# Attention output stored by accumulating DMAs onto the tokens in memory, so that the second scoring pass and the second feed-forward read one tensor

## The chip, the cores and the metric

The kernel runs on one core of one Trainium2 chip. The metric is the time of one execution on the device in microseconds. The time before is the median of three runs, 4940.31 us (4940.25 to 4942.61).

## The reference, cut to what matters

```python
def reference(x, ...):                       # x: 8 x 2048 x 256, float32
    x = x + 0.5 * ffn(layernorm(x), ...)     # first half block
    x = x + attention(layernorm(x), ...)     # 8 heads of 32 channels
    x = x + 0.5 * ffn(layernorm(x), ...)     # second half block, same weights

def ffn(x, w_router, W_qkv, W_out, g1, g2, W1, W2, W3):
    scores = x @ w_router                    # one number per token
    idx = top_k(scores, 128)                 # 128 of 2048 tokens per batch row
    x_sel = x[idx]                           # only these go through
    ...                                      # causal attention and gated FFN on 128 tokens
    return x with the rows idx replaced      # all other rows pass unchanged
```

The attention block's residual sum `x + attention(...)` is the one that the change moves. Each half block is also a pass over all 16384 tokens, since y = x + 0.5 * layernorm(x) for the tokens that are not picked.

## The kernel before, in words

Eight stages follow each other, each closed by a barrier of all engines (`cleared_semaphores`): `score_pass` s1, `pick_tokens` t1, `routed_ffn` f1, `project` pr, `attend` at, `score_pass` s2, `pick_tokens` t2, `routed_ffn` f2. The names of tiles begin with the stage (the profile drops the digit, so `s_x` is the tile x of s1 and s2).

**score_pass** (line 65) goes over 16 groups of 1024 tokens, four buffers deep. SP loads a group (1 MB, line 129), VectorE takes statistics and the router's product of each of its 8 tiles (lines 174 and 178) and then works out scale and bias in some 17 small dependent steps on 128x8 numbers (lines 184 to 205), ScalarE writes y (line 220) and issues its store (line 224). With `add` given, SP also loads the same group of a second tensor (line 132) and GpSimd adds it to the first in two halves (line 156); VectorE waits for each half. s1 is called without `add`; s2 adds `attention` to `after_ffn`.

**routed_ffn** (line 390) gathers the picked rows, 128 per batch row, with GpSimd's indirect DMAs (line 548), and with `add` a second gather and a GpSimd sum for each (lines 551 and 556). VectorE waits for the weights, which SP loads, and then for the rows (line 604). f1 is called without `add`, f2 with `attention`.

**attend** (line 1218) works in 64 units, 8 batch rows times 2 groups of four heads times 4 blocks of 512 queries. A unit has 16 cycles on TensorE (line 1676), one for each chunk c of 128 keys. A cycle computes the four heads' scores (line 1658), which ScalarE exponentiates into `probs` (line 1561, a ring of 8 chunks of 1 MB each), multiplies the chunk before with v (`pv`, line 1622) and computes one scores tile for the next units' row maxima (line 1589, reduced by VectorE in line 1462).

The sum of the exponentials over keys is shared. Chunks 13 and 15 are summed on TensorE. Ten others are added in pairs by accumulating DMAs from SBUF to SBUF, issued from GpSimd's queue (`start_pair`, line 1419): pairs (3,4), (5,6), (7,8), (9,10), (11,12). Pair d waits for TensorE to have passed chunk c of the pair (`pv_done`, line 1417). GpSimd adds what is left in eight adds of 128x2048 (line 1442), n = 0 to 7. The adds n = 2 to 6 take the results of pairs 0 to 4 and wait for their landing (`dma_added`, line 1430). GpSimd's order in a unit is written out: add 0, add 1, pairs 0 and 1, add 2, pair 2, add 3, pair 3, add 4, pair 4, adds 5, 6 and 7.

In cycle 3 of the next unit TensorE waits for the eighth add and closes the sum (`close_z`, line 1638). Turned and inverted, it scales the output in cycle 6 (`normalize`, line 1490), which fills `o`, of which there are two buffers, and raises `o_done`. SP waits for that and stores `o` into the tensor `attention` (`store`, line 1351): 256 KB in 512 rows of 128 channels, that is 512 B each, four to a partition. Between the stores SP issues the loads of queries, keys and values and the row maxima.

Of the kernel before, what the change touches and what calls it, by code (L numbers as in the profile page):

```python
# [15 lines left out]
P = 128  # L16
F32 = mybir.dt.float32
# [3 lines left out]
ALU = mybir.AluOpType  # L21
# [3 lines left out]
B, S, D = 8, 2048, 256  # L25
# [1183 lines left out]
RAW_CHUNKS = (13, 15)  # L1209
DMA_PAIRS = ((3, 4), (5, 6), (7, 8), (9, 10), (11, 12))  # L1210
DMA_BEFORE_ADD = (2, 2, 3, 4, 5)
CLOSE_Z_IN = 3
TURN_Z_IN = 4
TURN_O_IN = 6
# [3 lines left out]
def attend(nc, tag, qk, v_dram, out):  # L1218

    UQ = 512  # L1220
    NU = S // UQ
# [26 lines left out]
    with ExitStack() as ctx:  # L1248
# [63 lines left out]
        def _(sp):  # L1312
# [30 lines left out]
                                 .rearrange("a h (t q) -> a (h t) q", q=P),  # L1343
                                 max_row[first * QT:end * QT].bitcast(F32)).then_inc(max_in, 16)

            def store(unit, b, un):

                g, u = un // NU, un % NU
                sp.wait_ge(o_done, unit + 1)
                sp.sem_inc(load_turn, 1)  # L1350
                sp.dma_start(out[bass.ds(b * S + u * UQ, UQ), g * P:(g + 1) * P].rearrange("(t p) c -> p t c", p=P),
                             o[:, un % 2].rearrange("p t h d -> p t (h d)")).then_inc(o_out[un % 2], 16)

            load_q(0, 0)
            load_kv(0, 0)
            load_q(0, 1)
# [4 lines left out]
            def batch(b, first_batch=False, last=False):  # L1361

                for un in range(BU):
                    unit = b * BU + un
                    if un + 3 < BU or not last:

                        sp.wait_ge(scores, unit * TILES)
                        sp.sem_inc(load_turn, 1)
                        load_q(b + (un + 3) // BU, (un + 3) % BU)
                    if un == 0 and not first_batch:  # L1370

                        sp.wait_ge(pv_done, unit * NC)
                        sp.sem_inc(load_turn, 1)
                        load_kv(b, 1)
                    if un == NU and not last:

                        sp.wait_ge(pv_done, unit * NC)
                        sp.sem_inc(load_turn, 1)
                        load_kv(b + 1, 0)
                    if un > 0:  # L1380
                        store(unit - 1, b, un - 1)
                    elif not first_batch:
                        store(unit - 1, b - 1, BU - 1)
                    if un + 1 < BU or not last:
                        row_of_max(unit + 1, un + 1)
                if last:
                    store(b * BU + BU - 1, b, BU - 1)

            batch(0, first_batch=True)
            with sp.Fori(1, B - 1) as b:  # L1390
                batch(b)
            batch(B - 1, last=True)
            for k in range(2):
                sp.wait_ge(o_out[k], B * BU // 2 * 16)


        @block.gpsimd
        def _(pool):
# [7 lines left out]
            for first, end in ((0, HG - 1), (HG - 1, HG)):  # L1406
                to = SHIFT_AT[first]
                nc.gpsimd.memset(ks[to:to + 1, :, first:end].bitcast(F32), 1.0).then_inc(ones_row, 1)

            def batch(b, first_batch=False):  # L1410
                for un in range(BU):
                    unit = b * BU + un
# [7 lines left out]
                                            ).then_inc(dma_added[(un * ND + d) % 2], 16)  # L1420

                    for n in range(ADDS):
                        for d in range(ND):
                            if DMA_BEFORE_ADD[d] == n:
                                start_pair(d)
                        c = pool_chunks[n + 1]
                        paired = [d for d in range(ND) if DMA_PAIRS[d][1] == c]
                        if paired:
                            k = un * ND + paired[0]
                            pool.wait_ge(dma_added[k % 2], (b * (BU * ND // 2) + k // 2 + 1) * 16)  # L1430
                        else:
                            pool.wait_ge(exp_done, unit * TILES + c * HG + HG)
                        if n == 0:
                            if un > 1 or not first_batch:

                                pool.wait_ge(z_done, unit - 1)
                            a = probs[:, pool_chunks[0] % RING]
                        else:

                            pool.wait_ge(pool_added, unit * ADDS + n)  # L1440
                            a = acc
                        nc.gpsimd.tensor_tensor(acc, a, probs[:, c % RING], ALU.add).then_inc(pool_added, 1)  # L1442

            batch(0, first_batch=True)
            with pool.Fori(1, B) as b:
                batch(b)


        @block.vector
# [273 lines left out]
def macaron_block(nc, x, qU, qVt, qb, kU, kVt, kb, vU, vVt, vb, w_router, w_qkvT, w_outT, g1, g2, w1T, w2T, w3T,  # L1723
                  out):
    after_ffn = nc.dram_tensor("after_ffn", [B * S, D], F32).ap()
    attention = nc.dram_tensor("attention", [B * S, D], F32).ap()
    scores = nc.dram_tensor("router_scores", [P, P], F32).ap()
    qk = nc.dram_tensor("qk_parts", [B, 2, 2 * NG, P, S], F32).ap()
    v_dram = nc.dram_tensor("v_tokens", [B * S, D], F32).ap()
# [1 line left out]
    with nc.sbuf_tensor("picked", [P, B], U32) as picked:  # L1731
        score_pass(nc, "s1", x, None, w_router, after_ffn, scores)
        pick_tokens(nc, "t1", scores, picked[:])
        routed_ffn(nc, "f1", x, None, picked[:], *ffn_weights, after_ffn)
        project(nc, "pr", after_ffn, [(qU, qVt), (kU, kVt), (vU, vVt)], [qb, kb], vb, qk, v_dram)
        attend(nc, "at", qk, v_dram, attention)
        score_pass(nc, "s2", after_ffn, attention, w_router, out, scores)
        pick_tokens(nc, "t2", scores, picked[:])
        routed_ffn(nc, "f2", after_ffn, attention, picked[:], *ffn_weights, out)


# [32 lines left out]
```

## Time and profile before

| what | value |
|---|---|
| median of 3 runs | 4940.31 us |
| time of the profiled execution | 4941.97 us |
| its span, first to last instruction | 4940.2 us |
| mean granted TensorE clock | 0.933 |
| PE busy | 3962.8 us (80%) |
| DVE busy | 3256.7 us (66%) |
| ACT busy | 2839.3 us (57%) |
| POOL busy | 2797.0 us (57%) |
| DMA moved | 676.10 MB, mean 137 GB/s |

PE is TensorE, DVE VectorE, ACT ScalarE, POOL GpSimd, and SP the engine that issues most loads. The shares are means over the eight stages, of which attend takes some 3440 us, from 935 us to 4378 us of the span; the other stages have other limits. A wait is put down to the semaphore that came last. q0 is the DMA queue of the transfers that GpSimd issues, q1 that of SP, q10 that of ScalarE. All of them use the same 16 DMA engines.

### The profile page before, as it was taken

The numbers are of one execution on the slowest core, as the hardware profiler recorded it, in microseconds if no ns is written. First come the engines' busy times: TensorE is split into PE (matmuls) and PEld (weight loads), VectorE is DVE, ScalarE is ACT, GpSimd is POOL, SyncE is SP. The second block draws the span as 40 slices with busy tenths as digits, with TensorE's granted clock in tenths as the row PEclk, the third lists the DMA queues.
The fourth block names the chain that finished last, engine by engine and source line by source line (L and its number), as shares of the span: only waits on it lengthen the run. The fifth ranks groups of instructions, "written<-read, shape, count | busy, mean of one in ns | idle before, by whom it ended". The sixth has DMA issues, their size and how long they took to land. (4 is left out here: it accounts for less than half of the span.)

```text
span 4940.2 us, 69035 instructions
## 1 busy us (share of the span) xinstructions
PE 3962.8 (80%) x21362; PEld 1555.6 (31%) x21362; DVE 3256.7 (66%) x3736; ACT 2839.3 (57%) x5625; POOL 2797.0 (57%) x966
## 2 busy tenths in 40 slices
PE   0156476499999999999999999999999999930166
PEld 0134354133333333333333333333333333310144
DVE  8744365577767767776776776677677777549644
ACT  4143355266666666666666666666666666634043
POOL 0011000277777777777777777777777777753111
PEclk9999788699999999999999999999999999965599
DMA  6200499556676675766667575676657666467200
GB/s 222 76 29 5 149 353 328 113 124 139 131 157 134 136 154 110 158 127 144 146 132 151 108 163 122 138 157 128 144 119 162 129 138 129 92 192 246 78 5 5
DMA packets 316558, 676.10 MB, mean 137 GB/s; under 512 B 24780, under 2 KB 208608, under 8 KB 268832
## 3 DMA queue, kind: packets, MB, share of 16 engines
q0 software_dynamic: 48000, 340.81, 34.0%
q1 hardware_dynamic: 234624, 297.04, 20.9%
q10 hardware_dynamic: 33568, 33.69, 2.0%
q8 instruction: 191, 3.13, 0.3%
q14 instruction: 175, 1.43, 0.1%
HBM read 198.90 MB, written 136.48 MB: 68 GB/s over the span
## 5 line engine op out<-in xcount | busy, mean ns | idle before, releaser
L1462 DVE TENSOR_REDUCE at_part_max<-at_ps_max 128x4 f32<-128x2048 f32 x1024 | 2347.7, 2293 | 1022.6 <-PE at_ps_max L1589 1021.6
L1561 ACT ACTIVATE at_probs<-at_ps_s 128x512 f32<-128x512 f32 x4096 | 2233.4, 596 | 1045.3 <-PE at_ps_s L1658 989.8
L1442 POOL TENSOR_TENSOR at_pool_sum<-at_pool_sum,at_probs 128x2048 f32<-128x2048 f32 x448 | 2055.7, 4589 | 289.9 <-DMA at_probs<-at_probs 277.3
L1658 PE MATMUL at_ps_s<-at_qs,at_ks 97*128 97x512 f32 (+1 forms) x4096 | 1715.8, 472 | 72.0 <-ACT at_probs L1561 36.3
L1658 PEld LDWEIGHTS at_ps_s<-at_qs,at_ks 97*128 97x128 f32 (+1 forms) x4096 | 683.0, 188 | 1496.9 <-ACT at_probs L1561 1208.1
L1622 PE MATMUL at_ps_acc<-at_probs,at_v 128*32 128x512 f32 x8192 | 1098.0, 608 | 0.9 <-ACT at_probs L1561 0.9
L1589 PE MATMUL at_ps_max<-at_ks,at_qs 32*128 32x512 f32 x4096 | 525.2, 501 | 89.8 <-DVE at_part_max L1462 43.3
L1419 POOL DMA_DIRECT2D at_probs<-at_probs x320 | 282.0, 881 | 494.8 <-PE at_ps_acc L1622 465.9
L1442 POOL TENSOR_TENSOR at_pool_sum<-at_probs 128x2048 f32<-128x2048 f32 x64 | 292.2, 4566 | 98.7 <-ACT at_probs L1561 98.7
L1589 PEld LDWEIGHTS at_ps_max<-at_ks,at_qs 32*128 32x128 f32 x4096 | 198.1, 183 | 444.0 <-DVE at_part_max L1462 296.6
L238 PE MATMUL s_pt<-s_ident,s_sall 128*128 128x128 f32 x2 | 0.9, 447 | 359.5 <-DVE s_sall L205 359.5
L1622 PEld LDWEIGHTS at_ps_acc<-at_probs,at_v 128*32 128x32 f32 x8192 | 161.5, 108 | 257.3 <-issue 248.3
L1399 POOL MEMSET at_ones<- 128x128 f32 x1 | 0.2, 204 | 337.3 <-POOLq L62 337.3
L220 ACT ACTIVATE s_y<-s_x,s_small 128x256 f32<-128x256 f32 x256 | 129.2, 587 | 59.1 <-DVE s_small L201 59.1
L1187 PE MATMUL pr_pqk<-pr_xT,pr_w 128*128 128x512 f32 x256 | 132.3, 665 | 37.1 <-DVE pr_lo L1090 34.0
L565 POOL TENSOR_TENSOR f_att<-f_att,f_rowsum 128x1280 f32<-128x1280 f32 x16 | 49.5, 3096 | 172.3 <-DVE f_rowsum L650 172.3
L1630 PE MATMUL at_ps_misc<-at_probs,at_ones 128*32 128x512 f32 x1024 | 137.0, 607 | 0.0
L156 POOL TENSOR_TENSOR s_x<-s_x,s_add 128x1024 f32<-128x1024 f32 x32 | 74.3, 2342 | 100.5 <-DMA s_add<-attention 100.5
L752 ACT ACTIVATE f_att<-f_att,f_rowmax 128x128 f32<-128x128 f32 x256 | 98.7, 388 | 43.9 <-DVE f_rowmax L646 43.9
L1146 ACT ACTIVATE pr_hi<-pr_pqk,pr_bias 128x512 fp32r<-128x512 f32 x128 | 83.8, 683 | 60.4 <-PE pr_pqk L1187 60.1
L174 DVE BATCH_NORM_STATS2 s_stats<-s_x 128x6 f32<-128x256 f32 x256 | 107.9, 422 | 12.8 <-POOL s_x L156 8.0
L719 ACT ACTIVATE f_small<-f_small 128x4 f32<-128x4 f32 x4 | 0.8, 205 | 198.5 <-DVE f_small L612 198.5
(198 smaller groups left out, 2505.4 us busy)
## 6 DMA issues: line engine op xcount, KB each, us to landing
at_probs<-at_probs POOLq DMA_DIRECT2D x320, 1024.0 KB, 7.3
qk_parts<-pr_hi SPq DMA_DIRECT2D x32, 1024.0 KB, 6.5
qk_parts<-pr_lo SPq DMA_DIRECT2D x32, 1024.0 KB, 6.2
at_qs<-qk_parts SPq DMA_DIRECT2D x320, 64.0 KB, 1.9
at_ks<-qk_parts SPq DMA_DIRECT2D x80, 256.0 KB
s_x<-in_x SPq DMA_DIRECT2D x16, 1024.0 KB, 7.4
after_ffn<-s_y ACTq DMA_DIRECT2D x16, 1024.0 KB, 8.2
pr_x<-after_ffn SPq DMA_DIRECT2D x8, 2048.0 KB, 12.5
```

Of the source, the lines that this page charges most:

```text
L174: nc.vector.bn_stats(stats[:, k, t, :], xb[:, k, t, :]).then_inc(stats_done, 1)
L220: last = nc.scalar.activation(yb[:, k, t, :], xb[:, k, t, :], ACT.Identity, scale=sm[:, k, 0, t:t + 1], bias=sm[:, k, 1, t:t + 1])
L752: last = nc.scalar.activation(att[:, s, h], att[:, s, h], ACT.Exp, scale=ATT_SCALE, bias=rowmax[:, s, h:h + 1], accum_out=rowsum[:, s, h:h ...
L1187: nc.tensor.matmul(pqk[:, m, :], w[:, m // NG, m % NG, :], xT[:, n % 2, m % NG, :], start=True, stop=True).then_inc(qk_done, 1)
L1419: nc.gpsimd.dma_start(probs[:, c % RING], probs[:, a % RING], accum_op=ALU.add).then_inc(dma_added[(un * ND + d) % 2], 16)
L1442: nc.gpsimd.tensor_tensor(acc, a, probs[:, c % RING], ALU.add).then_inc(pool_added, 1)
L1462: nc.vector.reduce_max(part_max[:, :, t, c], ps_max[:], AX.X).then_inc(part_max_done, 1)
L1561: nc.scalar.activation(probs[:, c % RING, h], ps_s[:, j % 2], ACT.Exp, scale=SCALE).then_inc(exp_done, 1)
L1589: last = nc.tensor.matmul(ps_max[:, h], qs[rows, un % NQB, h, t * P:(t + 1) * P], ks[rows, un % BU // NU, h, c * 512:(c + 1) * 512], start ...
L1622: last = nc.tensor.matmul(ps_acc[h * DH:(h + 1) * DH, :], v[:, k // NU, c, h * DH:(h + 1) * DH], probs[:, c % RING, h], start=(c == 0), st ...
L1630: last = nc.tensor.matmul(ps_misc[h * DH:(h + 1) * DH, :], ones[:, 0:DH], probs[:, c % RING, h], start=(c == RAW_CHUNKS[0]), stop=False)
L1658: nc.tensor.matmul(ps_s[:, j % 2], ks[rows, g, h, c * P:(c + 1) * P], qs[rows, un % NQB, h, :], start=True, stop=True).then_inc(scores, 1)
```

## The change

In attend the store leaves SP and goes to GpSimd (`add_to_tokens`). It goes to `after_ffn` in place of `attention` and is an accumulating DMA: it adds the 256 KB to what lies in memory. It is issued ahead of add 3 of the next unit and ahead of pair 2, which stands at the same place. The last one is issued after GpSimd's loop, and GpSimd waits for all landings. s2 and f2 are then called without `add`, and the tensor `attention` is gone.

```diff
--- before.py
+++ after.py
@@ -1209,6 +1209,7 @@
 RAW_CHUNKS = (13, 15)
 DMA_PAIRS = ((3, 4), (5, 6), (7, 8), (9, 10), (11, 12))
 DMA_BEFORE_ADD = (2, 2, 3, 4, 5)
+STORE_BEFORE_ADD = 3
 CLOSE_Z_IN = 3
 TURN_Z_IN = 4
 TURN_O_IN = 6
@@ -1343,14 +1344,6 @@
                                  .rearrange("a h (t q) -> a (h t) q", q=P),
                                  max_row[first * QT:end * QT].bitcast(F32)).then_inc(max_in, 16)
 
-            def store(unit, b, un):
-
-                g, u = un // NU, un % NU
-                sp.wait_ge(o_done, unit + 1)
-                sp.sem_inc(load_turn, 1)
-                sp.dma_start(out[bass.ds(b * S + u * UQ, UQ), g * P:(g + 1) * P].rearrange("(t p) c -> p t c", p=P),
-                             o[:, un % 2].rearrange("p t h d -> p t (h d)")).then_inc(o_out[un % 2], 16)
-
             load_q(0, 0)
             load_kv(0, 0)
             load_q(0, 1)
@@ -1377,21 +1370,13 @@
                         sp.wait_ge(pv_done, unit * NC)
                         sp.sem_inc(load_turn, 1)
                         load_kv(b + 1, 0)
-                    if un > 0:
-                        store(unit - 1, b, un - 1)
-                    elif not first_batch:
-                        store(unit - 1, b - 1, BU - 1)
                     if un + 1 < BU or not last:
                         row_of_max(unit + 1, un + 1)
-                if last:
-                    store(b * BU + BU - 1, b, BU - 1)
 
             batch(0, first_batch=True)
             with sp.Fori(1, B - 1) as b:
                 batch(b)
             batch(B - 1, last=True)
-            for k in range(2):
-                sp.wait_ge(o_out[k], B * BU // 2 * 16)
 
 
         @block.gpsimd
@@ -1407,6 +1392,15 @@
                 to = SHIFT_AT[first]
                 nc.gpsimd.memset(ks[to:to + 1, :, first:end].bitcast(F32), 1.0).then_inc(ones_row, 1)
 
+            def add_to_tokens(unit, b, un):
+
+                g, u = un // NU, un % NU
+                pool.wait_ge(o_done, unit + 1)
+                pool.sem_inc(dma_turn, 1)
+                nc.gpsimd.dma_start(
+                    out[bass.ds(b * S + u * UQ, UQ), g * P:(g + 1) * P].rearrange("(t p) c -> p t c", p=P),
+                    o[:, un % 2].rearrange("p t h d -> p t (h d)"), accum_op=ALU.add).then_inc(o_out[un % 2], 16)
+
             def batch(b, first_batch=False):
                 for un in range(BU):
                     unit = b * BU + un
@@ -1420,6 +1414,10 @@
                                             ).then_inc(dma_added[(un * ND + d) % 2], 16)
 
                     for n in range(ADDS):
+                        if n == STORE_BEFORE_ADD and un > 0:
+                            add_to_tokens(unit - 1, b, un - 1)
+                        elif n == STORE_BEFORE_ADD and not first_batch:
+                            add_to_tokens(unit - 1, b - 1, BU - 1)
                         for d in range(ND):
                             if DMA_BEFORE_ADD[d] == n:
                                 start_pair(d)
@@ -1444,6 +1442,9 @@
             batch(0, first_batch=True)
             with pool.Fori(1, B) as b:
                 batch(b)
+            add_to_tokens(B * BU - 1, B - 1, BU - 1)
+            for k in range(2):
+                pool.wait_ge(o_out[k], B * BU // 2 * 16)
 
 
         @block.vector
@@ -1723,7 +1724,6 @@
 def macaron_block(nc, x, qU, qVt, qb, kU, kVt, kb, vU, vVt, vb, w_router, w_qkvT, w_outT, g1, g2, w1T, w2T, w3T,
                   out):
     after_ffn = nc.dram_tensor("after_ffn", [B * S, D], F32).ap()
-    attention = nc.dram_tensor("attention", [B * S, D], F32).ap()
     scores = nc.dram_tensor("router_scores", [P, P], F32).ap()
     qk = nc.dram_tensor("qk_parts", [B, 2, 2 * NG, P, S], F32).ap()
     v_dram = nc.dram_tensor("v_tokens", [B * S, D], F32).ap()
@@ -1733,10 +1733,10 @@
         pick_tokens(nc, "t1", scores, picked[:])
         routed_ffn(nc, "f1", x, None, picked[:], *ffn_weights, after_ffn)
         project(nc, "pr", after_ffn, [(qU, qVt), (kU, kVt), (vU, vVt)], [qb, kb], vb, qk, v_dram)
-        attend(nc, "at", qk, v_dram, attention)
-        score_pass(nc, "s2", after_ffn, attention, w_router, out, scores)
+        attend(nc, "at", qk, v_dram, after_ffn)
+        score_pass(nc, "s2", after_ffn, None, w_router, out, scores)
         pick_tokens(nc, "t2", scores, picked[:])
-        routed_ffn(nc, "f2", after_ffn, attention, picked[:], *ffn_weights, out)
+        routed_ffn(nc, "f2", after_ffn, None, picked[:], *ffn_weights, out)
 
 
 def kernel(L0_attn_x, L0_attn_Uq, L0_attn_Vq, L0_attn_bq, L0_attn_Uk, L0_attn_Vk, L0_attn_bk, L0_attn_Uv, L0_attn_Vv,
```

GpSimd's program in the second unit of attend, written out by the scheduler: eight adds (`at_pool_sum`), five pairs (`at_probs`). Before:

```order
L1442 TENSOR_TENSOR at_pool_sum<-at_probs 128x2048
L1442 TENSOR_TENSOR at_pool_sum<-at_pool_sum,at_probs 128x2048
L1419 DMA at_probs<-at_probs 128x2048 x2
L1442 TENSOR_TENSOR at_pool_sum<-at_pool_sum,at_probs 128x2048
L1419 DMA at_probs<-at_probs 128x2048
L1442 TENSOR_TENSOR at_pool_sum<-at_pool_sum,at_probs 128x2048
L1419 DMA at_probs<-at_probs 128x2048
L1442 TENSOR_TENSOR at_pool_sum<-at_pool_sum,at_probs 128x2048
L1419 DMA at_probs<-at_probs 128x2048
L1442 TENSOR_TENSOR at_pool_sum<-at_pool_sum,at_probs 128x2048 x3
```

Now:

```order
L1440 TENSOR_TENSOR at_pool_sum<-at_probs 128x2048
L1440 TENSOR_TENSOR at_pool_sum<-at_pool_sum,at_probs 128x2048
L1413 DMA at_probs<-at_probs 128x2048 x2
L1440 TENSOR_TENSOR at_pool_sum<-at_pool_sum,at_probs 128x2048
L1400 DMA after_ffn<-at_o 128x4x128
L1413 DMA at_probs<-at_probs 128x2048
L1440 TENSOR_TENSOR at_pool_sum<-at_pool_sum,at_probs 128x2048
L1413 DMA at_probs<-at_probs 128x2048
L1440 TENSOR_TENSOR at_pool_sum<-at_pool_sum,at_probs 128x2048
L1413 DMA at_probs<-at_probs 128x2048
L1440 TENSOR_TENSOR at_pool_sum<-at_pool_sum,at_probs 128x2048 x3
```

The new row, the store from `at_o` onto `after_ffn`, stands between add 2 and pair 2. Every pair and add behind it in the unit comes after it on GpSimd, and pair 2 comes after it in queue q0.

GpSimd's program in the second feed-forward, from its last constant to the first product. Before:

```order
L543 AFFINE_SELECT f_head_of<-f_head_half 128x8
L548 DMA f_xs<-after_ffn,picked 128x256
L551 DMA f_ads<-attention,picked 128x256
L548 DMA f_xs<-after_ffn,picked 128x256
L551 DMA f_ads<-attention,picked 128x256
L548 DMA f_xs<-after_ffn,picked 128x256
L551 DMA f_ads<-attention,picked 128x256
L548 DMA f_xs<-after_ffn,picked 128x256
L551 DMA f_ads<-attention,picked 128x256
L556 TENSOR_TENSOR f_xs<-f_xs,f_ads 128x256 x4
L548 DMA f_xs<-after_ffn,picked 128x256
L551 DMA f_ads<-attention,picked 128x256
```

Now:

```order
L543 AFFINE_SELECT f_head_of<-f_head_half 128x8
L548 DMA f_xs<-after_ffn,picked 128x256 x8
L565 TENSOR_TENSOR f_att<-f_att,f_rowsum 128x1280 x4
L571 DMA out<-f_row,picked 16384x256 x4
L565 TENSOR_TENSOR f_att<-f_att,f_rowsum 128x1280 x4
```

Eight gathers and eight adds are gone, and the gathers of the second four batch rows follow the first four at once.

SP's program in the loop of attend, around one of its stores. Before:

```order
L1322 DMA at_qs<-qk_parts 32x3x512
L1325 DMA at_qs<-qk_parts 32x2x512 x2
L1351 DMA attention<-at_o 128x4x128
L1339 REGISTER_ALU
L1342 DMA at_qs<-at_max_row 1x12x128
L1342 DMA at_qs<-at_max_row 1x4x128
```

Now:

```order
L1323 DMA at_qs<-qk_parts 32x3x512
L1326 DMA at_qs<-qk_parts 32x2x512 x2
L1340 REGISTER_ALU
L1343 DMA at_qs<-at_max_row 1x12x128
L1343 DMA at_qs<-at_max_row 1x4x128
```

The store's row is gone; the loads of queries ahead of it and the two row-maximum DMAs behind it are as they were.

## Rows read from the trace of the kernel before

**Rows 1.** Busy time by stretch: s1 with t1, s2 with t2, attend.

```profile
core 0: us, PE busy (x) PEld busy (x) DVE busy (x) ACT busy (x) POOL busy (x), PEclk, DMA share, GB/s
0.00:243.20 243.20, 15.73 (x67) 14.71 (x67) 194.87 (x860) 74.99 (x151) 1.73 (x12) 1.00 0.44 148
4378.80:4661.80 283.00, 15.74 (x67) 14.71 (x67) 230.87 (x860) 73.71 (x150) 75.78 (x41) 0.50 0.55 186
...
1000.00:4300.00 3300.00, 3226.18 (x17869) 1119.39 (x17869) 2328.01 (x1175) 2218.27 (x4145) 2520.36 (x804) 1.00 0.64 137
```

**Rows 2.** Waits within attend: who waited for whom, us in total, times, longest us.

```profile
POOL at_probs L1419 <- PE at_ps_acc L1622: 465.9, 155, 5.6
...
PEld at_ps_misc L1638 <- POOL at_pool_sum L1442: 11.8, 8, 7.2
```

**Rows 3.** Tiles s_x and s_y: ns min/median/max, then first and last start.

```profile
L156 POOL TENSOR_TENSOR s_x<-s_x,s_add x32: 2331/2343/2360, 4389.1 to 4551.9; 128x1024 f32<-128x1024 f32 x32
...
L224 ACTq DMA_DIRECT2D after_ffn<-s_y x16: 378/442/503, 21.2 to 161.2; - x16
...
L224 ACTq DMA_DIRECT2D out<-s_y x16: 378/444/464, 4410.9 to 4579.9; - x16
```

**Rows 4.** Small VectorE steps of the score passes, of 128x8 numbers.

```profile
L185 DVE TENSOR_TENSOR s_small<-s_stats x32: 171/173/2262, 14.0 to 4572.7; 128x8 f32<-128x8 f32 x32
```

**Rows 5.** Timeline of POOL and DVE, starts of f1 and f2: start, us, what.

```profile
243.24 0.21 POOL L532 MEMSET f_ones<- 128x128 f32 x1 [75.18 <-POOLq L62]
...
257.60 0.17 DVE L607 TENSOR_TENSOR f_small<-f_stats 128x4 f32<-128x4 f32 x1
...
4661.80 0.21 POOL L532 MEMSET f_ones<- 128x128 f32 x1 [75.16 <-POOLq L62]
...
4677.75 0.17 DVE L607 TENSOR_TENSOR f_small<-f_stats 128x4 f32<-128x4 f32 x1
```

**Rows 6.** Timeline of POOL in one unit of attend, pair 1 to add 7.

```profile
2572.31 0.86 POOL L1419 DMA_DIRECT2D at_probs<-at_probs  x1 [5.41 <-PE at_ps_acc L1622]
2575.02 4.56 POOL L1442 TENSOR_TENSOR at_pool_sum<-at_pool_sum,at_probs 128x2048 f32<-128x2048 f32 x1 [1.84 <-DMA at_probs<-at_probs]
2579.53 0.86 POOL L1419 DMA_DIRECT2D at_probs<-at_probs  x1
...
2586.65 4.55 POOL L1442 TENSOR_TENSOR at_pool_sum<-at_pool_sum,at_probs 128x2048 f32<-128x2048 f32 x1 [0.82 <-DMA at_probs<-at_probs]
2591.15 0.85 POOL L1419 DMA_DIRECT2D at_probs<-at_probs  x1
...
2598.89 9.21 POOL L1442 TENSOR_TENSOR at_pool_sum<-at_pool_sum,at_probs 128x2048 f32<-128x2048 f32 x2 [1.62 <-DMA at_probs<-at_probs]
```

**Rows 7.** Timelines: PE after that unit; POOL and PE at a tight unit's end.

```profile
2610.99 1.04 PE L1638 MATMUL at_ps_misc<-at_pool_sum,at_ones 128*32 128x512 f32 x8
...
1427.00 9.21 POOL L1442 TENSOR_TENSOR at_pool_sum<-at_pool_sum,at_probs 128x2048 f32<-128x2048 f32 x2 [2.38 <-DMA at_probs<-at_probs]
...
1436.26 1.06 PE L1638 MATMUL at_ps_misc<-at_pool_sum,at_ones 128*32 128x512 f32 x8 [0.56 <-POOL at_pool_sum L1442]
```

**Rows 8.** Issues by tile or line, and their DMA to landing (us min/median/max).

```profile
L1419 POOL DMA_DIRECT2D at_probs<-at_probs x320: 838/875/1198, 967.2 to 4353.1; - x160
DMA to landing us min/median/max: 6.9/7.3/11.8
...
L1351 SPq DMA_DIRECT2D attention<-at_o x64: 378/423/431, 1027.0 to 4375.4; - x64
DMA to landing us min/median/max: 2.3/7.4/10.5
...
q0 software_dynamic: 48000, 340.81, 34.0%
```

**Rows 9.** End of attend and start of s2: timelines of SP and POOL.

```profile
4375.43 0.38 SPq L1351 DMA_DIRECT2D attention<-at_o  x1
...
4378.83 0.21 POOL L145 MEMSET s_ones<- 128x128 f32 x1 [9.55 <-POOLq L62]
```

## Prediction

> **What bounds the kernel now.** I first looked at busy time by stretch, since the means of the page mix stages. In attend TensorE is busy 3226 of 3300 us, GpSimd 2520 and VectorE 2328 [rows 1]: TensorE sets the pace, and everything else has to be in time for it. s1 with t1 and s2 with t2 are the same program but for the second tensor: 243.2 us against 283.0 us, and GpSimd's 75.8 us of work stands only in the second [rows 1]. Next I read who waits for whom in attend. GpSimd waits 465.9 us for TensorE before it starts pairs, so it has air; but TensorE has already waited for GpSimd's sum 8 times [rows 2], so in some units it has none. That is the wait on which the change hangs, and it needs the timeline of a unit.
>
> In the unit of rows 6 pair 1 starts at 2572.31 as soon as TensorE allows. Pair 2 goes out at 2579.53 and add 4 waits for its landing until 2586.65; pair 4 goes out at 2591.15 and add 6 waits for it until 2598.89; add 7 ends at 2608.10 [rows 6]. TensorE comes to close_z at 2610.99 [rows 7]: 2.9 us of slack. Another unit has none: adds 6 and 7 end at 1436.21 and TensorE, 0.56 us idle, starts close_z at 1436.26 [rows 7]. I took this difference in the same views for all 64 units: five have 0.12 us or less of slack, 14 more 0.5 to 2.4 us, 40 have 2.8 to 4.0 us and five over 7 us. The shortest are mostly units beside which SP loads the 4 MB of keys and values of a head group.
>
> **The second scoring pass (gain).** It loses 16 loads of 1 MB, GpSimd's 32 halves of 2.34 us [rows 3] and VectorE's waits for them. What is left is s1, line by line. Between first and last store of y s1 takes 161.2 - 21.2 = 140.0 us, s2 4579.9 - 4410.9 = 169.0 us [rows 3]. VectorE's small steps fall too: they have a median of 173 ns but take up to 2262 ns [rows 4], the long ones in s2 beside GpSimd's sums. From its first instruction to that of f2, s2 with t2 takes 4661.80 - 4378.83 = 283.0 us [rows 5, 9]; the same point in f1 stands at 243.24 us of the span [rows 5]. That is 39.7 us less, and as the kernel's start lies in it too I take **-40 us**. Bounds: 29 us (the stores' stretch alone) and 41 us.
>
> **The second feed-forward (gain).** Eight gathers and eight sums go. From the first instruction to the first statistics step f1 takes 257.60 - 243.24 = 14.4 us, f2 4677.75 - 4661.80 = 16.0 us [rows 5]. f1, without `add`, waits for the weights, and so will f2: **-1.6 us**. The second four rows are gathered beside other work and give nothing.
>
> **What the store costs in attend.** 64 issues of 0.42 us go from SP [rows 8], which bounds nothing: nothing. On GpSimd 64 issues come. Call D the time by which pair 2 lands later in the unit. It has two parts: the issue itself, which pair 2 and add 3 wait for, and the store's data, which run ahead of pair 2 on the same queue. Its own wait for `o_done` is no part: `o` is written in cycle 6, pair 1 waits for cycle 7, and the store comes 5 us later still, behind add 2. Behind it on GpSimd are pairs 2 to 4 and adds 3 to 7, and TensorE's close_z waits for the last.
> - Issue: a pair takes 0.875 us in 128 pieces of 8 KB [rows 8]. The store has 512 pieces. If the count costs nothing it is 0.9 us, if it is all that counts 3.5 us. I take 1.6 us, nearer to the lower end, as I expect a fixed part to be most of the 0.875 us.
> - Data: q0 was busy 34.0% of the span for 320 pairs [rows 8], 0.34 x 4940 / 320 = 5.2 us each; a quarter of the bytes is 1.3 us. Small pieces cost more; the old plain store took at most 10.5 us to land where the undisturbed one took 2.3 us [rows 8], so I bound it by 4 us and take 2 us.
>
> The data move while pair 2 is being issued, so the two overlap and the longer counts: **D = 2.0 us**, ends 0.9 and 4.0 us. The old store's share of the DMA engines beside pair 1 goes away, worth a few tenths at most; I leave it out.
>
> What D costs I worked out unit by unit: every pair and add starts at the latest of GpSimd's last end, TensorE's time and the landing it waits for, each pair lands as long after its issue as it did, and whenever add 7 ends after close_z's time, TensorE and all that follows moves by the difference. A late end of one unit also delays pair 0 of the next. The total over 64 units: D = 1.0 gives 5 us, 1.5 gives 9, 2.0 gives 13, 2.5 gives 25, 3.0 gives 48, 3.5 gives 76, 4.0 gives 104. Up to about 2.2 us only the tight units pay; above that 57 units pay the rest in full, 57 us per us. The cover of the cheap part is thus the 2 to 3 us that GpSimd is ahead of TensorE. I add 2 us for the tight units, where the store must share the DMA engines with the key loads: **+15 us**.
>
> **The end of attend.** SP issued the last store at 4375.43 and s2 began at 4378.83 [rows 9]. GpSimd issues more slowly and memory is read before it is written: +0.5 to +4 us, **+2 us**.
>
> **Sum**: 4941.97 - 40 - 1.6 + 15 + 2 = 4917.4 us against the profiled execution's own time of 4941.97 us (1.7 us over the median, its span 4940.2 us), so **4916 us** against the median 4940.3 us.
>
> A rule that bears on it: pairs land 7.3 us after issue [rows 8]. The Trainium skill (DMA: Bandwidth & Descriptors, Anatomy of one DMA) fits a GpSimd-issued DMA as 2.0 us plus bytes over 436 GB/s, which is 4.4 us for 1 MB, so the trace does not agree for accumulating ones. By that fit the store's data would take 0.6 us, D would be the issue alone and the sum some 4 us lower.
>
> **The rivals.**
> - *Hidden* (chance 0.22): issue and data both stay under 1.5 us. For it: GpSimd's air of 465.9 us [rows 2]. Against: four times the pieces. Time: 4916 - 8 = 4908 us, down to 4903.
> - *In order* (0.17): a queue takes its transfers one after the other, so that the store's data do not begin until its issue is done and pair 2's not before they end: D = 1.6 + 1.3 = 2.9 us, 43 us in attend in place of 13. Then 4916 + 30 = 4946 us, within 10 us of before. Before, the store ran on q1 beside the pairs. The Trainium skill (same page, Queues, rings and completion order) says that an engine takes turns between queues but starts the descriptors of one queue in order; the wait for the landing of pair 2 will show it, and no row here does.
> - *GpSimd becomes the bound* (0.20), the other side: the 512 pieces are made at the rate of the pair's 128, 3.5 us of issue, or each small piece reads memory before the next starts. At D = 3.5 to 4 us it is 76 to 104 us in attend: 4916 + 63 to 91 = 4979 to 5007 us. It decides from D = 2.9 us on, the loss then being over the 42 us gained. For it: 5 units already have no slack. Against: an issue with fixed work in it.
> - *No gain in s2* (0.03): VectorE's statistics would bound it, not the second tensor. Against: s1 in the same trace. Time: 4956 us.
>
> **How the numbers follow.** The forecast, D between 1.5 and 2.5 us, has 0.38. A measurement can tell 0.2%, about 10 us, from no change. Faster by more: forecast and hidden, with part of in order, 0.66. Within 10 us: most of in order, 0.11. Slower: the bound case, no gain and the rest, 0.23. The range runs from 4902 us (D = 0.9 and the upper bound of s2's gain) to 4975 us, which leaves out the longer part of the bound case.
>
> **What would show it.** In the profile after: s2 with t2 in 243 us; y stores 9.3 us apart; GpSimd's issue of the store near 1.6 us; pair 2's landing some 2 us later against pair 1; TensorE's wait for GpSimd at close_z in 10 to 20 units, 20 us in all; most unit periods unchanged. Store issues near 3 us, or close_z waiting in most units, would make the prediction wrong and the bound case right; pair 2 landing over 2.5 us later beside a short issue would mean that data in order is what counts.

## The result, and the profile after

| what | before | after |
|---|---|---|
| median, us | 4944.57 (20 runs, 4940.25 to 4950.23) | 4953.34 (20 runs, 4942.49 to 4963.14) |
| time of the profiled execution, us | 4941.97 | 4961.93 |
| its span, us | 4940.2 | 4960.3 |
| mean granted TensorE clock | 0.933 | 0.929 |

The ratio of after to before is 1.0019, with a 95% interval of 1.0012 to 1.0025: 8.8 us more, just inside the 0.2% that I had set as no change. The forecast was 4916 us and faster. The spans of the two profiled executions are 20.1 us apart, 11 us more than the medians, so the accounts below are of one execution that lies in the slower half of after's spread.

**The gain came.** Busy time by stretch of after: s2 with t2, then f2, then attend (columns as in [rows 1]):

```profile
4440.30:4681.40 241.10, 15.74 (x67) 14.71 (x67) 194.80 (x860) 73.72 (x150) 1.49 (x9) 0.50 0.45 149
4681.40:4960.30 278.90, 176.12 (x848) 108.41 (x848) 112.24 (x189) 106.03 (x353) 41.72 (x30) 0.85 0.06 19
1000.00:4360.00 3360.00, 3260.40 (x17884) 1127.96 (x17876) 2326.60 (x1175) 2221.71 (x4147) 2602.82 (x868) 0.99 0.66 134
```

s2 with t2 takes 241.1 us where it took 283.0 us, and GpSimd does 1.5 us of work there in place of 75.8. The tile s_y and one of VectorE's small steps, as [rows 3, 4]:

```profile
L224 ACTq DMA_DIRECT2D out<-s_y x16: 378/444/459, 4460.2 to 4599.5; - x16
```

```profile
L185 DVE TENSOR_TENSOR s_small<-s_stats x32: 170/172/173, 14.3 to 4592.4; 128x8 f32<-128x8 f32 x32
```

The stores of y are (4599.5 - 4460.2) / 15 = 9.3 us apart, and the step that took up to 2262 ns beside GpSimd's sums now never takes more than 173.

**The loss is in attend.** Worked out for all 64 units, pair 1 of the first to pair 1 of the last takes 3418.2 us where it took 3361.2: +57.0 us. The timeline of POOL in an ordinary unit, pair 1 to add 7, to be laid beside [rows 6]:

```profile
2596.69 0.86 POOL L1413 DMA_DIRECT2D at_probs<-at_probs  x1 [5.42 <-PE at_ps_acc L1623]
2599.34 4.57 POOL L1440 TENSOR_TENSOR at_pool_sum<-at_pool_sum,at_probs 128x2048 f32<-128x2048 f32 x1 [1.79 <-DMA at_probs<-at_probs]
2603.85 1.31 POOL L1400 DMA_DIRECT2D after_ffn<-at_o  x1
2604.65 1.42 POOL L1413 DMA_DIRECT2D at_probs<-at_probs  x1
2605.22 5.44 POOL L1440 TENSOR_TENSOR at_pool_sum<-at_pool_sum,at_probs 128x2048 f32<-128x2048 f32 x1
2609.72 1.77 POOL L1413 DMA_DIRECT2D at_probs<-at_probs  x1
2613.24 4.56 POOL L1440 TENSOR_TENSOR at_pool_sum<-at_pool_sum,at_probs 128x2048 f32<-128x2048 f32 x1 [1.75 <-DMA at_probs<-at_probs]
2617.75 0.87 POOL L1413 DMA_DIRECT2D at_probs<-at_probs  x1
2620.59 4.56 POOL L1440 TENSOR_TENSOR at_pool_sum<-at_pool_sum,at_probs 128x2048 f32<-128x2048 f32 x1 [1.97 <-DMA at_probs<-at_probs]
2626.05 9.23 POOL L1440 TENSOR_TENSOR at_pool_sum<-at_pool_sum,at_probs 128x2048 f32<-128x2048 f32 x2 [0.90 <-DMA at_probs<-at_probs]
```

From pair 1 to add 4 it is 2613.24 - 2596.69 = 16.55 us, against 2586.65 - 2572.31 = 14.34 in [rows 6]. Over the 64 units the mean went from 14.52 to 16.38 us, so that D, as the prediction calls it, is 1.86 us. Pair 2 is issued only 0.4 us later than before, because it begins 0.8 us after the store, while the store's own issue still runs; the other 1.45 us is its landing.

The tile at_o, then q0's row of the page, as in [rows 8]:

```profile
L1400 POOL DMA_DIRECT2D after_ffn<-at_o x64: 1294/1316/1653, 1029.8 to 4432.5; - x64
DMA to landing us min/median/max: 4.3/4.7/5.9
```

```profile
q0 software_dynamic: 81408, 356.54, 36.9%
```

The issue takes 1.32 us (1.6 taken, 0.9 to 3.5 bounded). Who waited for whom within attend, as in [rows 2], here with the matmul's own wait too (before, that one stood at 6.8 us, 2 times):

```profile
POOL at_probs L1413 <- PE at_ps_acc L1623: 391.5, 97, 5.7
...
PEld at_ps_misc L1639 <- POOL at_pool_sum L1440: 42.4, 21, 8.2
PE at_ps_misc L1639 <- POOL at_pool_sum L1440: 28.7, 10, 7.3
```

TensorE waited for the sum ten times instead of two (6 to 7 us of each total is the last unit's end). The other nine are the units 4, 8, 12, 20, 28, 36, 44, 52 and 56, all of them beside loads of keys and values, and all of them with 1.3 us of slack or less before. Their periods are 54.3 to 61.1 us, where all units but those at the loop's edge take 52.9. The end of unit 12, timelines of POOL and PE:

```profile
1652.00 9.18 POOL L1440 TENSOR_TENSOR at_pool_sum<-at_pool_sum,at_probs 128x2048 f32<-128x2048 f32 x2 [0.72 <-DMA at_probs<-at_probs]
...
1658.21 1.06 PE L1623 MATMUL at_ps_acc<-at_probs,at_v 128*32 128x512 f32 x8
...
1661.23 1.06 PE L1639 MATMUL at_ps_misc<-at_pool_sum,at_ones 128*32 128x512 f32 x8 [1.96 <-POOL at_pool_sum L1440]
...
1662.90 0.78 PE L1590 MATMUL at_ps_max<-at_ks,at_qs 32*128 32x512 f32 x4
...
1664.76 1.84 PE L1623 MATMUL at_ps_acc<-at_probs,at_v 128*32 128x512 f32 x8
...
1667.64 0.51 PE L1590 MATMUL at_ps_max<-at_ks,at_qs 32*128 32x512 f32 x4
1668.73 1.06 PE L1623 MATMUL at_ps_acc<-at_probs,at_v 128*32 128x512 f32 x8
```

TensorE idles 1.96 us. (Below, a stall is the time by which close_z starts later than it does after the same matmul in an ordinary unit, 0.2 us more than the idle time in the brackets.) Then, though it waits for nobody, its eight matmuls with v take 1.84 us where they took 1.06 before the stall and take 1.06 again four us later. The stretches of that moment (the column behind the engines is PEclk):

```profile
1655.00:1661.00 6.00, 4.26 (x25) 1.17 (x24) 3.81 (x2) 2.98 (x6) 5.92 (x2) 1.00 0.05 17
1661.00:1667.00 6.00, 5.77 (x26) 1.93 (x27) 2.29 (x1) 2.65 (x5) 5.92 (x3) 0.72 0.01 3
1667.00:1690.00 23.00, 22.79 (x127) 8.28 (x125) 17.16 (x10) 16.25 (x30) 17.36 (x8) 1.00 0.75 143
```

The granted clock falls behind the stall: 0.72 is the mean of a stretch in which it was for 3.4 us at its lower level (1.2 GHz) and for the rest at the upper (2.4 GHz). Summed over the clock records of attend, the lower level was granted for 27.3 us in 5 stretches before and for 99.0 us in 13 after. The 27.3 us of before stand at five of the loop's edges, where TensorE idles too, and after has 27.3 us there as well. The other eight stretches, 71.7 us, each come with a stall at close_z; of the nine only unit 28, stalled by 1.4 us, has none. In the units 8, 44 and 56 the clock fell 0.3 to 0.6 us before TensorE went on.

What such a stretch costs can be read from the time that TensorE takes from close_z to the 270th matmul behind it, against ordinary units: 1.2, 2.7, 4.2 and 5.5 us for stretches of about 3.4, 6.8, 10.2 and 13.7 us, 0.4 of their length, 29 us for all eight. The stalls themselves come to 23 us, where before had 0.9. The rest is at the five edges of the loop, TensorE's timeline at the first of them, before and after:

```profile
1798.06 1.22 PE L1658 MATMUL at_ps_s<-at_qs,at_ks 97*128 97x512 f32 x2 [3.43 <-issue]
```

```profile
1813.57 1.22 PE L1659 MATMUL at_ps_s<-at_qs,at_ks 97*128 97x512 f32 x2 [4.44 <-issue]
```

It idled 3.4 to 3.7 us at each and now idles 4.4 to 5.3 us, 6 us more in all; no run shows why. Together 22 + 29 + 6 = 57 us, the 57 measured.

**The rest.** The end of attend, timelines of POOL and SP, as in [rows 9]:

```profile
4432.46 1.32 POOL L1400 DMA_DIRECT2D after_ffn<-at_o  x1 [6.67 <-DVE at_o L1491]
...
4440.30 0.20 POOL L145 MEMSET s_ones<- 128x128 f32 x1 [6.51 <-POOLq L62]
```

From the last store to s2 it is 7.8 us in place of 3.4: +4.4. And the start of f2, as in [rows 5]:

```profile
4681.39 0.21 POOL L532 MEMSET f_ones<- 128x128 f32 x1 [75.16 <-POOLq L62]
...
4696.11 0.17 DVE L607 TENSOR_TENSOR f_small<-f_stats 128x4 f32<-128x4 f32 x1
```

14.7 us where it was 16.0; f2 as a whole takes 0.5 us more than before, at a granted clock of 0.85 against 0.86. The sum of the parts, -41.9 + 57.0 + 4.4 + 0.5 = +20.0, is the difference of the spans.

### The profile page after: what moved, and what is told of

The parts are those of the page before. It is cut to its first block and busy times, and to the rows that moved or that the text cites. A ratio compares the mean times of both kernels' runs of the same rounds, so it can differ in the third digit from the quotient of the medians.

```text
span 4960.3 us, 68926 instructions
## 1 busy us (share of the span) xinstructions
PE 3994.8 (81%) x21362; PEld 1563.8 (32%) x21362; DVE 3219.6 (65%) x3736; ACT 2841.3 (57%) x5625; POOL 2793.6 (56%) x982
## 3 DMA queue, kind: packets, MB, share of 16 engines
q0 software_dynamic: 81408, 356.54, 36.9%
## 5 line engine op out<-in xcount | busy, mean ns | idle before, releaser
L1440 POOL TENSOR_TENSOR at_pool_sum<-at_pool_sum,at_probs 128x2048 f32<-128x2048 f32 x448 | 2093.1, 4672 | 360.0 <-DMA at_probs<-at_probs 347.6
L1413 POOL DMA_DIRECT2D at_probs<-at_probs x320 | 337.5, 1055 | 397.7 <-PE at_ps_acc L1623 391.5
L1090 DVE SCALAR_TENSOR_TENSOR pr_lo<-pr_pqk,pr_bias,pr_hi 128x512 fp32r<-128x512 f32 x128 | 88.6, 744 | 41.7 <-ACT pr_hi L1146 35.8
```

The costliest lines, as they stand in the source:

```text
L1413: nc.gpsimd.dma_start(probs[:, c % RING], probs[:, a % RING], accum_op=ALU.add).then_inc(dma_added[(un * ND + d) % 2], 16)
```

## The experiments

The theory: the second tensor was worth some 42 us, and the store costs as much again, nearly all of it in the units beside key loads, by a late pair 2 that lets TensorE stall and by the clock that falls with the stall. The rivals: GpSimd's issue time is the cost, not the queue; the loss is in all units; a stall costs its own length and the clock is chance. All ratios are to the kernel before on the same chip.

**Each half alone.** The gain without the accumulating store: SP stores as before but onto `after_ffn`, replacing what is there.

```diff
- attend(nc, "at", qk, v_dram, attention)
+ attend(nc, "at", qk, v_dram, after_ffn)
```

> The store stays a plain one from SP, but into after_ffn, and s2 and f2 read one tensor. The residual sum with after_ffn is left out. Both theories: attend as before, s2 with t2 42 us shorter, f2's start 1 us shorter: 4944.6 - 43 = 4902 us. If s2's gain were not additive (for instance taken back in f2 by the clock), above 4910 us.

Measured: 4897.81 us (before 4943.15), ratio 0.9909 (0.9893 to 0.9924). -45.3 us; attend's 64 units take 3363.5 us, 2.3 more than before.

The store without the gain: the changed attend, and s2 and f2 still read a second tensor.

```diff
- score_pass(nc, "s2", after_ffn, None, w_router, out, scores)
+ score_pass(nc, "s2", after_ffn, v_dram, w_router, out, scores)
```

> The changed attend alone: accumulating store from GpSimd, but s2 and f2 add a second tensor as before (v_tokens in place of attention, so the value is another). Theory: attend's loss is whole, stalls 20 us and clock 20 to 35 us and 4 us at its end: 4944.6 + 45 to 60 = 4990 to 5005 us. Rival (loss comes from s2's side, or the two parts interact): under 4975 us.

Measured: 4994.96 us, ratio 1.0109 (1.0093 to 1.0124), +51.8 us. In its profile ten stretches of low clock come to 68.3 us and the stalls to 20.4 us. The halves add up: -45.3 + 51.8 = +6.5, against +8.8 for the whole. So the gain is there in full, and attend gives it back.

**The place of the store.** Behind all pairs:

```diff
-STORE_BEFORE_ADD = 3
+STORE_BEFORE_ADD = 6
```

> The changed kernel with the store issued ahead of add 6, behind pair 4, in place of ahead of add 3 and pair 2. Theory (the store delays pair 2 and with it the eighth add; in the units beside key loads, which had no slack, TensorE then stalls at close_z and its clock falls after each stall): no pair is behind the store here and add 6 waits for pair 4's landing anyway, so attend is as long as before, 5 to 7 low-clock stretches, total 4944.6 - 42 (s2) + 4 (end of attend) = 4907 us, 4903 to 4915. Rival (the accumulating store costs wherever it is issued, by GpSimd's time or by its traffic): as the changed kernel, 4950 us or more.

Measured: 4906.84 us, ratio 0.9926 (0.9913 to 0.9940). The same store, as long to issue, costs 9 us of attend instead of 57 when nothing stands behind it in q0 in that unit. It is the changed kernel but for this one number, and faster than both.

Right behind pair 2, at the same place among the adds:

```diff
-                        if n == STORE_BEFORE_ADD and un > 0:
-                            add_to_tokens(unit - 1, b, un - 1)
...
                         for d in range(ND):
                             if DMA_BEFORE_ADD[d] == n:
                                 start_pair(d)
+                        if n == STORE_BEFORE_ADD and un > 0:
+                            add_to_tokens(unit - 1, b, un - 1)
```

> The changed kernel with the store issued right behind pair 2, still ahead of add 3, in place of right before pair 2. GpSimd does the same work at the same place; only the order in the queue is turned. If what counts is the store's data ahead of pair 2's (its pieces start 1.8 us after its issue, and pair 2's start only when they end), pair 2 lands as before, stalls at close_z beside key loads shrink to what the slower add 3 costs (under 1 us each), total 4907 to 4920 us. Rival (GpSimd's own time for the issue, 1.3 us and the slower add behind it): 4940 to 4953 us.

Measured (before 4941.53): 4910.01 us, ratio 0.9932 (0.9919 to 0.9946). GpSimd issues exactly what it issued before add 3, only in the other order, and 40 us are gone (31.5 us under the kernel before in place of 8.8 over it). Add 4 is 0.36 us later than in the kernel before instead of 1.86. Tile at_o of this run:

```profile
L1400 POOL DMA_DIRECT2D after_ffn<-at_o x64: 1303/1546/1669, 1031.3 to 4378.6; - x64
...
DMA to landing us min/median/max: 4.3/8.7/10.3
```

The issue is even longer (1.55 us), and it is now the store that waits: it lands after 8.7 us in place of 4.7. This settles the first rival: what counts is who stands first in the queue, not how long GpSimd issues.

**What makes the store's data slow.** The same DMA from the same place, without adding, so that it replaces what it should be added to:

```diff
-                    o[:, un % 2].rearrange("p t h d -> p t (h d)"), accum_op=ALU.add).then_inc(o_out[un % 2], 16)
+                    o[:, un % 2].rearrange("p t h d -> p t (h d)")).then_inc(o_out[un % 2], 16)
```

> The changed kernel with a plain store from GpSimd at the same place (the residual sum is left out). If accumulation makes the data slow (65 ns a piece of 512 B against about 31 ns for plain ones on SP's queue), the data part of the delay halves: the late landing of pair 2 falls from 1.5 us to about 0.5 us, total 4925 to 4940 us. If the number of pieces in the issue is all that counts, it stays within 4 us of the changed kernel.

Measured: 4909.39 us, ratio 0.9939 (0.9925 to 0.9952), lower than I had expected. It is 32.1 us under the kernel before, where the plain store from SP was 45.3 us under it: from GpSimd, ahead of pair 2, a plain store costs some 13 us, the adding one 54 us. Tile at_o, then q0's row of the page:

```profile
L1400 POOL DMA_DIRECT2D after_ffn<-at_o x64: 812/814/1121, 1028.8 to 4380.8; - x64
...
DMA to landing us min/median/max: 2.8/3.1/4.5
```

```profile
q0 software_dynamic: 52736, 356.54, 35.3%
```

Two things fall: the issue, from 1.32 to 0.81 us, and the packets of q0, from 81408 to 52736 for the same bytes. The 28672 that are missing are 448 for each of the 64 stores: one of 512 packets of 512 B has become one of 64 packets of 4 KB. In the trace the small packets take 65 ns each, 512 x 65 / 16 = 2.1 us on sixteen engines, the large ones 0.22 us each, 0.9 us. The cut is not all of it: the plain store that SP issued before was cut into 512 packets of 512 B too, and in its trace they take 27 ns each (median). So an adding packet takes more than twice the time of a plain one of its size, and GpSimd's plain store has fewer packets besides. How much of the 2.1 us comes from the one and how much from the other was not separated.

**The place of the loss.** SP's loads of keys and values are spread over three units, 1, 2 and 1 MB, instead of 4 MB in one:

```diff
+PIECES = ((0,), (1, 3), (2,))
...
-                    if un == 0 and not first_batch:
+                    if un % NU < len(PIECES) and (un >= NU and not last or un < NU and not first_batch):
...
-                        load_kv(b, 1)
+                        load_kv(b + un // NU, 1 - un // NU, PIECES[un % NU])
```

> The changed kernel with the 4 MB of keys and values of a head group loaded as 1 MB, 2 MB and 1 MB beside three units in place of 4 MB beside one. Theory (the loss is in the nine units beside key loads that had no slack): their pairs 0 and 1 land earlier, most of the nine stalls and low-clock stretches go, total 4915 to 4930 us. Rival (the store costs TensorE in every unit, by contention or by clock): no change from 4953 us.

Measured: 4908.52 us, ratio 0.9932 (0.9918 to 0.9945). The store stands where the change put it, outside the units 4, 8, ... 56 add 4 is 1.8 to 1.9 us later than in the kernel before, and only one unit stalls, by 0.8 us. In its profiled execution attend takes 7.8 us more than before, in place of 57. Nearly all of the loss thus came from nine units of 64.

Both remedies together, late store and spread loads:

> Both cures: store ahead of add 6, and loads in three parts. Theory: no stall at close_z but the one that ends attend, total 4897 to 4903 us. Rival (the late store had taken back all there was): as with the late store alone, 4907 us.

Measured: 4904.56 us, ratio 0.9924 (0.9911 to 0.9938), a little above what was expected and not to be told from the late store alone. The late store alone had left stalls of 4 us in attend, one of them followed by 3.4 us of low clock, so that there was little for the second remedy to take away.

**More slack.** TensorE closes the sum a cycle later:

```diff
-CLOSE_Z_IN = 3
-TURN_Z_IN = 4
-TURN_O_IN = 6
+CLOSE_Z_IN = 4
+TURN_Z_IN = 5
+TURN_O_IN = 7
```

> The changed kernel with close_z, turn_z and turn_o one cycle later (4, 5, 7 in place of 3, 4, 6). Theory: every unit has 3.1 us more slack at close_z; the stalls of 1.3 to 2.7 us beside key loads vanish and with them the clock's falls; total 4944.6 - 42 + 4 = 4907 us, or a few less, as before too had stalls. Rival (attend lost its time to something else, the ring's release to ScalarE or later key loads): stays within 5 us of the changed kernel, 4950 us.

Measured: 4926.80 us, ratio 0.9966 (0.9952 to 0.9979), half of what was expected. GpSimd used up part of the slack: add 7 ended 38.9 us after pair 1 instead of 37.75, and units 12 and 56 still stalled by 2.1 and 3.9 us, and the clock fell with both. TensorE also idled 4.4 to 6.3 us at the loop's edges. A later deadline does not take the store out of the queue.

**The price of a stall.** The kernel before, with a sum of nobody's numbers on GpSimd ahead of add 7 in eight units that have no key load beside them, short and long:

```diff
+                        if n == ADDS - 1 and un == 5:
+                            pool.wait_ge(z_done, unit)
+                            spare = pool_sum[:, (un + 1) % 2]
+                            nc.gpsimd.tensor_tensor(spare[:, :4], spare[:, :4], spare[:, :4], ALU.add).then_inc(spare_added, 1)
+                            pool.wait_ge(spare_added, b * 2 + 1)
+                            nc.gpsimd.tensor_tensor(spare[:, :2], spare[:, :2], spare[:, :2], ALU.add).then_inc(spare_added, 1)
+                            pool.wait_ge(spare_added, b * 2 + 2)
```

(long; the short one has the first sum alone)

> The kernel before with one more sum of 128x2048 (4.56 us, of numbers nobody reads) on GpSimd ahead of add 7 in the units 5, 13, ... 61, eight of 64, none of them beside a key load. Their slack at close_z is 26.1 us in sum in the trace of before, so that TensorE must stall 8 x 4.6 - 26.1 = 10.7 us there, 1.3 us each. If a stall costs its own length, about 11 us over before (4954). If each one also brings a stretch of low granted clock, as the stalls of the changed kernel do (about 4 us each), 11 + 32 = 43 us over before (4986). In the runs so far stalls of 0.3 to 1.3 us brought few of them, so I expect nearer to the first, 10 to 20 us over before.

> As the run with the small delay, but with a second sum of half the width (2.3 us) behind the first, in the same eight units: stalls of 8 x 6.9 - 26.1 = 29.1 us in sum, 3.6 us each, as long as those of the changed kernel in the units beside key loads. If a stall costs its own length: 29 us over before (4973). If each of these also brings low granted clock at 4 us: 29 + 32 = 61 us over before (5005), with eight more stretches of low clock in attend than before has. I expect the second, 50 to 70 us.

Measured: short 4945.81 us (before 4944.49), ratio 1.0005 (0.9995 to 1.0014); long 4976.95 us, ratio 1.0072 (1.0051 to 1.0092). Both stalled less than planned, as the extra sum, with one tile for both its operands, took 3.6 us and not 4.56, and both came out below what was expected of them: 1.3 us over before in place of 10 to 20, and 32.5 us in place of 50 to 70. Timeline of PE in unit 29 of the short one:

```profile
2554.69 1.06 PE L1628 MATMUL at_ps_acc<-at_probs,at_v 128*32 128x512 f32 x8
2556.45 1.06 PE L1644 MATMUL at_ps_misc<-at_pool_sum,at_ones 128*32 128x512 f32 x8 [0.69 <-POOL at_pool_sum L1448]
...
2559.55 1.07 PE L1628 MATMUL at_ps_acc<-at_probs,at_v 128*32 128x512 f32 x8
```

and of the long one, then the stretch behind its stall:

```profile
2569.60 1.07 PE L1646 MATMUL at_ps_misc<-at_pool_sum,at_ones 128*32 128x512 f32 x8 [1.80 <-POOL at_pool_sum L1450]
...
2573.04 1.92 PE L1630 MATMUL at_ps_acc<-at_probs,at_v 128*32 128x512 f32 x8
```

```profile
2571.00:2577.00 6.00, 6.00 (x28) 2.28 (x26) 2.75 (x2) 3.77 (x8) 5.92 (x2) 0.72 0.00 0
```

| run, its profiled execution | units made to stall | each, us | followed by low clock | low clock in attend | attend, 64 units |
|---|---|---|---|---|---|
| before | none | - | - | 27.3 us | 3361.2 us |
| short | 8 | 0.5 to 1.0 in six, less in two | none | 23.9 us | 3363.5 us |
| long | 8 | 2.0 to 3.0 | 7 of 8 | 71.7 us | 3397.9 us |

The long one lost 36.7 us in attend: 19 us in stalls (18 us of them in the eight units) and, measured behind close_z as above, 18 us by the low clock. This was set up in the kernel before, with no store on GpSimd and no key load beside those units, and it shows the same: a stall of 2 us costs more than its length, and the fall of the clock is brought by it. The short stalls brought no fall.

**The store twice.** The accumulating store issued a second time, onto a tensor nobody reads:

```diff
+                nc.gpsimd.dma_start(
+                    twice[bass.ds(b * S + u * UQ, UQ), g * P:(g + 1) * P].rearrange("(t p) c -> p t c", p=P),
+                    o[:, un % 2].rearrange("p t h d -> p t (h d)"), accum_op=ALU.add).then_inc(o_out[un % 2], 16)
```

> The changed kernel with each accumulating store issued twice, the second time onto a tensor that nobody reads. Pair 2 should then be late by about 3.9 us against before instead of 2.0 (1.3 us of issue and 2 us of data more, partly beside each other), and the unit-by-unit recurrence of the prediction gives about 100 us in attend instead of 13, nearly every unit stalling by about 1 us. With stalls at their own length: 87 us over the changed kernel, about 5040. If each of some 57 stalls also brought low clock at 4 us it would be over 5200. I expect 5030 to 5070, since stalls of 1 us have brought few low stretches so far.

Measured: 5056.92 us, ratio 1.0231 (1.0214 to 1.0248). Add 4 came 3.75 us later than in the kernel before. The time is in the range, but made up otherwise. Attend takes 145.6 us more: stalls of up to 6.3 us in some 40 units came to 84 us, the low clock behind fifteen of them cost 46 us, and the loop's edges 15 us more than before, where TensorE now idled 6.2 to 6.4 us. The stalls of 0.6 to 1.8 us were followed by none of it, the fifteen longer ones all were.

## Why the prediction was wrong

- *The second scoring pass*, -40 us: -41.9. Right, by the step that read it off s1.
- *The second feed-forward*, -1.6 us: its start gained 1.2 us. Right; with the clock of the later part f2 came out even.
- *D = 2.0 us*: 1.86 over all units. Right, though by other parts and so partly by luck. The issue took 1.32 us and not 1.6, but a second issue overlaps it and only 0.4 us reached pair 2. The data, bounded at 1.3 to 4 us and taken as 2, were ahead of pair 2 in the queue: 1.45 us.
- *The rival "in order"* had its mechanism right, as the store behind pair 2 shows, which alone took 40 us off. Its size, D = 2.9 us, was too large because it put the whole issue in front of the data.
- *"Up to about 2.2 us only the tight units pay", +15 us*: **this is the step that failed**; attend took 57.0 us more. Who pays was right: nine units, all tight. What they pay was mis-sized twice. First, D is not one number. In the 14 units 4, 8, ... 56, where the loads run, add 4 came 2.5 us later and add 7 ended 2.7 us later, in the units without loads 1.7 and 1.5 us. Stalls of 22 us more than before follow, near the 25 us that the recurrence gives for D = 2.5, and not 13 + 2. Second, and larger, the recurrence moved TensorE by the length of the stall and by nothing else. With each stall of 2 us or more the granted clock fell to its lower level, for 3.4 to 13.7 us, and that cost 29 us of the 57. A further 6 us, at the loop's edges, were in no term either; their cause stays open. The row that could have warned me was there: [rows 7] shows a tight unit, and the clock records of the same trace show five low stretches in attend, at the loop's edges where TensorE idles for 3.4 to 3.7 us. The eight waits that I counted in [rows 2] were those of the weight loads; the matmuls themselves had waited twice. The mean of 1.00 in [rows 1] hides the low stretches, and the sum has no term for the clock. The sign that I named, waits at close_z in 10 to 20 units and 20 us in all, came nearly true (ten waits, 28.7 us with the last unit's end), while the price of such a wait was wrong.
- *The end of attend*, +2 us: +4.4, just outside its bounds of 0.5 to 4.
- *"GpSimd becomes the bound"* did not happen: the issue is not near 3 us, and ordinary units keep their 52.9 us. Its result, a gain that attend gives back, came by a smaller delay and a dearer stall.

Why the medians lie closer than the profiled executions was not measured. Which stalls bring a fall of the clock varies between executions (in two of the runs above, stalls of 2.1 and 2.5 us brought none), and the wider spread of the runs after fits that.

## What to carry to other kernels

Before moving a DMA into a queue, look at who is queued behind it and at the units with the least slack, not at the mean: here the same store cost 57 us in attend ahead of a transfer on which TensorE's deadline hangs, and 4 to 9 us behind it. Price a stall of a busy TensorE from 2 us upwards as more than its length, since the clock can fall with it (here for another 1.2 to 5.5 us each). And where one resource is short in a few units only, take the load away there (other place, spread loads) before doubting the gain.

## What the runs showed of the hardware

- An accumulating DMA onto memory was cut into 512 packets of 512 B where the plain one of the same shape from GpSimd had 64 of 4 KB: issue 1.32 against 0.81 us, landing 4.7 against 3.1 us. SP's plain one had 512 of 512 B as well; an adding packet of that size took 65 ns, a plain one 27 ns. Accumulating from SBUF to SBUF kept packets of 8 KB.
- Two DMA issues of GpSimd overlap by some 0.5 us, and its own sum beside them takes 5.44 us in place of 4.56.
- Data of one queue start in the order of issue, seen from both sides: pair 2 late behind the store (in unit 40 the store's packets ran from 1.9 to 4.1 us after its issue, pair 2's from 3.5 us on), the store at 8.7 us behind pair 2. The Trainium skill (DMA: Bandwidth & Descriptors, Two DMAs through the same engine are not ordered) says that within one queue of one DMA engine descriptors start in order, but may complete out of it; the starts in this case agree.
- In all the profiled executions together, 38 of 40 stalls of TensorE of 1.9 us and more came with 3.4 to 13.7 us of the lower clock, and of the shorter ones a single one, of 1.3 us (unit 56 of the run with the store behind pair 2, 3.4 us).
